# Moving the loads of the weights and the condition behind the first two chunks of x

## The chip, the cores and the metric

The kernel runs on one core of one Trainium2 chip. The metric is the time of one execution on the device in microseconds (us), the median of several runs; lower is better. The engines that matter here are TensorE (PE, with its weight loads as PEld), VectorE (DVE), ScalarE (ACT), SyncE (SP), and the 16 DMA engines of the core.

## The reference

The input x has 128 samples of 128 steps of 512 float32 numbers. A condition (128 x 512) goes through two dense layers and gives one gate of 512 numbers for each sample.

```python
h = silu(cond @ W1.T + b1)                 # 128 x 512
gate = sigmoid(h @ W2.T + b2)[:, None, :]  # one value per sample and feature
# a Haar transform of x over the 128 steps (log2(128) levels), its details and its
# average times gate, then the inverse transform
y = x + (x + inverse_haar(gate * haar(x))) # the gate is the same for all steps
```

The gate doesn't depend on the step, so the transform and its inverse cancel, and the result is `x * (2 + gate)`. That is what the kernel computes: one factor for each sample and feature, and one multiply over 33.6 MB of x that are read and written once.

## The kernel before

**The stream.** x is cut into 2 groups (g) of 64 samples. In each group the 128 partitions are 64 samples times 2 halves of the steps, and 8 chunks (s) of 8 steps each go over them. A chunk is 128 x 4096 float32, 2.1 MB. The tile `ring` has 8 slots, so the whole first group fits into it. SyncE (`block.sync`) issues the loads: first W1, the condition and W2 (L100 to L102), then the 8 chunks of group 0 (L104) without a wait, then the 8 chunks of group 1 (L109), each after the store of the chunk that held its slot (`chunk_stored`). All of these lie in one DMA queue, SP's, which the profile calls q1. VectorE multiplies chunk after chunk by `factor` in place (L218), each after its load (`chunk_loaded`). ScalarE issues the store of each chunk once it is scaled (L182), in its own DMA queue, q10. These stores hold 33.6 MB.

**The gate.** Before VectorE can scale the first chunk, `factor` has to be there. It comes from a chain over three engines. TensorE waits for the condition, turns it by 4 transposes (L126), then turns W1 by 16 (L132), and multiplies (`hidden_sum`, L140, 32 instructions). ScalarE takes the sigmoid (L171) while TensorE turns W2 (L149). VectorE copies turned tiles out of PSUM (L191, L194, L208) and forms `hidden` (L201). TensorE then forms `gate_sum` for group 0 and for group 1 (L157 for the bias, L160 for the product), ScalarE takes two sigmoids (L176), and VectorE adds 2 (L211, `factor`). VectorE and ScalarE run their instructions in the order written, so no chunk is scaled or stored ahead of this chain. The two biases are loaded in ScalarE's queue (L165, L166).

The parts that the change and the steps of the prediction touch:

Of the kernel before, what the change touches and what calls it, by code (L numbers as in the profile page):

```python
# [1 line left out]

# [8 lines left out]
CHUNK_STEPS = 8  # L31
GROUPS = 2
SLOTS = 8
DMA_DONE = 16


def gated_residual_program(nc, x, cond, w1, b1, w2, b2, out):
    B, N, D = x.shape
    BLOCKS = D // P
    SAMPLES = B // GROUPS  # L40
    assert B == P and D == BLOCKS * P and N == GROUPS * SLOTS * CHUNK_STEPS and GROUPS >= 2

    x_parts = x.rearrange("(g q) (h n) d -> g (q h) n d", g=GROUPS, h=GROUPS)
    out_parts = out.rearrange("(g q) (h n) d -> g (q h) n d", g=GROUPS, h=GROUPS)

    with ExitStack() as ctx:
        def sbuf(name, shape):
            return ctx.enter_context(nc.sbuf_tensor(name, shape, F32))
# [4 lines left out]
        def sem(name):  # L53
            return ctx.enter_context(nc.semaphore(name))


        ring = sbuf("ring", [P, SLOTS, CHUNK_STEPS, D])

# [27 lines left out]
        gate_summed, gate_set, factor_set = sem("gate_summed"), sem("gate_set"), sem("factor_set")  # L86
        chunk_loaded = [sem(f"chunk_loaded{s}") for s in range(SLOTS)]
        chunk_scaled = sem("chunk_scaled")
        chunk_stored = [sem(f"chunk_stored{s}") for s in range(SLOTS)]

        block = ctx.enter_context(nc.Block())

        def chunk(parts, g, s):

            return parts[bass.ds(g, 1), :, s * CHUNK_STEPS:(s + 1) * CHUNK_STEPS, :].rearrange("g p n d -> (g p) n d")

        @block.sync
        def _(sp):

            sp.dma_start(w1_rows[:, :, :], w1.rearrange("(p t) k -> p t k", t=BLOCKS)).then_inc(w1_loaded, DMA_DONE)  # L100
            sp.dma_start(cond_rows[:, :], cond).then_inc(cond_loaded, DMA_DONE)
            sp.dma_start(w2_rows[:, :, :], w2.rearrange("(t p) k -> p t k", p=P)).then_inc(w2_loaded, DMA_DONE)  # L102
            for s in range(SLOTS):
                sp.dma_start(ring[:, s, :, :], chunk(x_parts, 0, s)).then_inc(chunk_loaded[s], DMA_DONE)  # L104
            with sp.Fori(1, GROUPS) as g:
                for s in range(SLOTS):

                    sp.wait_ge(chunk_stored[s], g * DMA_DONE)
                    sp.dma_start(ring[:, s, :, :], chunk(x_parts, g, s)).then_inc(chunk_loaded[s], DMA_DONE)  # L109

# [130 lines left out]
```

## Time and profile before

| | before |
|---|---|
| median of 3 runs | 168.21 us (167.97 to 169.08) |
| span of the profiled execution | 166.7 us |
| time of the profiled execution beside its span | not recorded apart from the span |
| busy share of the span | DVE 47%, PE 14%, PEld 9%, ACT 2%, POOL 1% |
| DMA | 69.47 MB, mean 417 GB/s over the span |
| HBM read, written | 35.92 MB, 33.55 MB |

The span is the time from the first to the last instruction of the profiled execution. Against it stand the sums below; the median of the runs is 1.5 us above it. The page divides the span into 40 slices of 4.17 us; the digit in the DMA row is the mean busy share of the 16 DMA engines in tenths:

```profile
DVE  0160180019999999997809154280915428000000
DMA  5999999999999999999999999999999999999995
```

VectorE is busy without a break only from slice 9 on, and has gaps again in the second group. The DMA engines are at nine tenths or more in every slice but the first and the last.

### The profile page before, as it was taken

The numbers are of one execution on the slowest core, as the hardware profiler recorded it, in microseconds if no ns is written. First come the engines' busy times: TensorE is split into PE (matmuls) and PEld (weight loads), VectorE is DVE, ScalarE is ACT, GpSimd is POOL, SyncE is SP. The second block draws the span as 40 slices with busy tenths as digits, with TensorE's granted clock in tenths as the row PEclk, the third lists the DMA queues.
The fourth block names the chain that finished last, engine by engine and source line by source line (L and its number), as shares of the span: only waits on it lengthen the run. The fifth ranks groups of instructions, "written<-read, shape, count | busy, mean of one in ns | idle before, by whom it ended". The sixth has DMA issues, their size and how long they took to land.

```text
span 166.7 us, 361 instructions
## 1 busy us (share of the span) xinstructions
PE 23.7 (14%) x88; PEld 15.6 (9%) x88; DVE 78.3 (47%) x30; ACT 3.6 (2%) x7; POOL 0.8 (1%) x7
## 2 busy tenths in 40 slices
PE   0479619960000000000000000000000000000000
PEld 0479613320000000000000000000000000000000
DVE  0160180019999999997809154280915428000000
ACT  0000500110000000000000000000000000000000
POOL 2000000000000000000000000000000000000000
PEclk9999965997555555555555555555555555555555
DMA  5999999999999999999999999999999999999995
GB/s 167 313 457 440 421 421 429 433 437 433 413 437 429 429 437 440 425 425 429 437 429 437 433 425 433 429 433 433 437 433 425 433 429 429 437 433 433 429 429 236
DMA packets 5570, 69.47 MB, mean 417 GB/s; under 512 B 705, under 2 KB 705, under 8 KB 1346
## 3 DMA queue, kind: packets, MB, share of 16 engines
q1 hardware_dynamic: 3120, 35.91, 51.3%
q10 hardware_dynamic: 2450, 33.56, 47.1%
HBM read 35.92 MB, written 33.55 MB: 417 GB/s over the span
## 4 chain that ended last, share of the span: by engine, by line
DMA 41%; DVE 26%; PE 13%; ACT 2%; issue 2%; SPq 0%; DVEq 0%; ACTq 0%
DMA out<-ring 27%; DVE ring L218 22%; DMA ring<-in_x 11%; PE gate_sum L160 5%; PE hidden_sum L140 3%; DMA cond_rows<-in_cond 3%; PE turned L132 2%; PE gate_sum L157 2%; DVE w_t L208 1%; DVE hidden L201 1%; ACT L171 1%; ACT hidden_sigmoid L171 1%; PE turned_cond L126 1%; DVE factor L211 0%; DVE w_t L194 0%
## 5 line engine op out<-in xcount | busy, mean ns | idle before, releaser
L218 DVE TENSOR_TENSOR ring<-ring,factor 128x4096 f32<-128x4096 f32 x16 | 70.1, 4421 | 33.3 <-DMA ring<-in_x 33.0
L160 PE MATMUL gate_sum<-w_t,hidden 128*128 128x512 f32 x16 | 8.8, 702 | 0.0
L211 DVE TENSOR_SCALAR factor<-gate 128x1024 f32<-128x1024 f32 x1 | 0.7, 694 | 12.6 <-ACT gate L176 12.6
L140 PE MATMUL hidden_sum<-cond_t,w_t 128*128 128x128 f32 x32 | 5.5, 351 | 0.9 <-DVE w_t L194 0.9
L201 DVE SCALAR_TENSOR_TENSOR hidden<-hidden_sum,b_cols,hidden_sigmoid 128x256 f32<-128x256 f32 x4 | 1.7, 478 | 8.3 <-ACT hidden_sigmoid L171 8.3
L140 PEld LDWEIGHTS hidden_sum<-cond_t,w_t 128*128 128x128 f32 x32 | 5.3, 264 | 1.2 <-issue 1.2
L191 DVE COPY cond_t<-turned_cond 128x512 f32<-128x512 f32 x1 | 0.7, 692 | 7.8 <-PE turned_cond L126 7.8
L160 PEld LDWEIGHTS gate_sum<-w_t,hidden 128*128 128x128 f32 x16 | 3.5, 229 | 6.0 <-issue 6.0
L157 PE MATMUL gate_sum<-b_row,ones_row 1*128 1x512 f32 x4 | 3.2, 881 | 4.9 <-DVE w_t L208 4.9
L132 PE MATMUL turned<-identity,w_rows 128*128 128x128 f32 x16 | 3.6, 421 | 0.0
L132 PEld LDWEIGHTS turned<-identity,w_rows 128*128 128x128 f32 x16 | 3.4, 230 | 0.0
L194 DVE COPY w_t<-turned 128x512 f32<-128x512 f32 x4 | 2.8, 692 | 0.6 <-PE turned L132 0.6
L208 DVE COPY w_t<-turned 128x512 f32<-128x512 f32 x4 | 2.5, 681 | 0.0
L149 PE MATMUL turned<-identity,w_rows 128*128 128x128 f32 x16 | 2.1, 283 | 0.0
L126 PE MATMUL turned_cond<-identity,cond_rows 128*128 128x128 f32 x4 | 1.1, 428 | 6.6 <-DMA cond_rows<-in_cond 6.6
L149 PEld LDWEIGHTS turned<-identity,w_rows 128*128 128x128 f32 x16 | 2.0, 208 | 0.0
L171 ACT ACT_TABLE_LOAD x1 | 1.3, 1283 | 17.6 <-PE hidden_sum L140 17.6
L176 ACT ACTIVATE gate<-gate_sum 128x512 f32<-128x512 f32 x2 | 1.2, 597 | 15.5 <-PE gate_sum L160 15.5
L157 PEld LDWEIGHTS gate_sum<-b_row,ones_row 1*128 1x128 f32 x4 | 0.8, 244 | 5.8 <-issue 5.8
L126 PEld LDWEIGHTS turned_cond<-identity,cond_rows 128*128 128x128 f32 x4 | 0.7, 216 | 6.6 <-issue 6.6
L171 ACT ACTIVATE hidden_sigmoid<-hidden_sum,b_cols 128x128 f32<-128x128 f32 x4 | 1.1, 368 | 0.0
L117 POOL TENSOR_SCALAR_AFFINE_SELECT identity<-identity 128x128 f32<-128x128 f32 x1 | 0.3, 294 | 0.1
(6 smaller groups left out, 0.8 us busy)
## 6 DMA issues: line engine op xcount, KB each, us to landing
ring<-in_x SPq DMA_DIRECT2D x16, 2048.0 KB, 18.2
out<-ring ACTq DMA_DIRECT2D x16, 2048.0 KB, 34.8
w_rows<-in_L_cond_W SPq DMA_DIRECT2D x2, 1024.0 KB, 6.8
cond_rows<-in_cond SPq DMA_DIRECT2D x1, 256.0 KB, 5.3
b_cols<-in_L_cond_b ACTq DMA_DIRECT2D x1, 2.0 KB, 5.2
b_row<-in_L_cond_b ACTq DMA_DIRECT2D x1, 2.0 KB
```

The lines of the kernel that those rows point to most:

```text
L126: last = pe.transpose(turned_cond[:, c * B:(c + 1) * B], cond_rows[:, c * P:(c + 1) * P], identity[:, :])
L132: last = pe.transpose(turned[c][:, t * P:(t + 1) * P], w1_rows[:, t, c * P:(c + 1) * P], identity[:, :])
L140: last = pe.matmul(hidden_sum[:, t, :], w1_t[:, c, t, :], cond_t[:, c, :], start=(c == 0), stop=(c == BLOCKS - 1))
L149: last = pe.transpose(turned[t][:, m * P:(m + 1) * P], w2_strided[:, m, t, :], identity[:, :])
L157: pe.matmul(gate_sum[g][:, :], ones_row[:, :], b2_row[:, :], start=True, stop=False)
L160: last = pe.matmul(gate_sum[g][:, :], samples, w2_t[:, t, :], start=False, stop=(t == BLOCKS - 1))
L171: act.activation(hidden_sigmoid[:, t, :], hidden_sum[:, t, :], ACT.Sigmoid, bias=b1_cols[:, t:t + 1]).then_inc(sigmoid_set, 1)
L176: act.activation(gate[:, g, :], gate_sum[g][:, :], ACT.Sigmoid).then_inc(gate_set, 1)
L194: dve.tensor_copy(w1_t[:, c, :, :].rearrange("k t p -> k (t p)"), turned[c][:, :]).then_inc(w1_t_set, 1)
L201: dve.scalar_tensor_tensor(out=hidden[:, t, :, :], in0=hidden_sum[:, t, :].unsqueeze(2).to_broadcast([P, B, GROUPS]), scalar=b1_cols[:, t: ...
L208: dve.tensor_copy(w2_t[:, t, :], turned[t][:, :]).then_inc(w2_t_set, 1)
L218: dve.tensor_tensor(ring[:, s, :, :], ring[:, s, :, :], factor_steps, ALU.mult).then_inc(chunk_scaled, 1)
```

## The change

SyncE now issues the loads of chunks 0 and 1 of group 0 first, then W1, the condition and W2, and then chunks 2 to 7. The instructions are the same, with the same sizes, semaphores and queue; only their order on SyncE differs. Nothing changes on the other engines.

```diff
@@ -31,6 +11,7 @@
 CHUNK_STEPS = 8
 GROUPS = 2
 SLOTS = 8
+AHEAD = 2
 DMA_DONE = 16
@@ -97,10 +78,12 @@
         @block.sync
         def _(sp):
 
+            for s in range(AHEAD):
+                sp.dma_start(ring[:, s, :, :], chunk(x_parts, 0, s)).then_inc(chunk_loaded[s], DMA_DONE)
             sp.dma_start(w1_rows[:, :, :], w1.rearrange("(p t) k -> p t k", t=BLOCKS)).then_inc(w1_loaded, DMA_DONE)
             sp.dma_start(cond_rows[:, :], cond).then_inc(cond_loaded, DMA_DONE)
             sp.dma_start(w2_rows[:, :, :], w2.rearrange("(t p) k -> p t k", p=P)).then_inc(w2_loaded, DMA_DONE)
-            for s in range(SLOTS):
+            for s in range(AHEAD, SLOTS):
                 sp.dma_start(ring[:, s, :, :], chunk(x_parts, 0, s)).then_inc(chunk_loaded[s], DMA_DONE)
             with sp.Fori(1, GROUPS) as g:
                 for s in range(SLOTS):
```

## Rows read from the trace of the kernel before

**Rows 1.** The page's DMA queues: packets, MB, share of the 16 engines' span.

```profile
q1 hardware_dynamic: 3120, 35.91, 51.3%
q10 hardware_dynamic: 2450, 33.56, 47.1%
```

**Rows 2.** Windows: stretch, its length, busy us of PE, PEld, DVE, ACT, POOL, PEclk, DMA share, GB/s.

```profile
0.00:42.40 42.40, 23.68 (x88) 15.62 (x88) 12.81 (x16) 3.62 (x7) 0.84 (x7) 0.88 0.96 395
42.40:48.00 5.60, 0.00 (x0) 0.00 (x0) 5.60 (x2) 0.00 (x0) 0.00 (x0) 0.50 0.99 424
48.00:164.80 116.80, 0.00 (x0) 0.00 (x0) 59.88 (x14) 0.00 (x0) 0.00 (x0) 0.50 1.01 431
```

**Rows 3.** Chain of waits from the condition to `gate_sum`: start, length in us, what.

```profile
1.17 5.32 DMA cond_rows<-in_cond
6.63 1.09 PE turned_cond L126 x4
7.72 3.43 PE turned L132 x16
12.01 5.50 PE hidden_sum L140 x32
24.33 2.04 PE gate_sum L157 x2
31.41 1.05 PE gate_sum L157 x2
32.47 3.65 PE gate_sum L160 x8
```

**Rows 4.** Timeline, the scaling and storing: start, length, engine, line, operation, count.

```profile
37.79 26.10 DVE L218 TENSOR_TENSOR ring<-ring,factor 128x4096 f32<-128x4096 f32 x6 [0.33 <-DVE factor L211]
...
42.38 0.39 ACTq L182 DMA_DIRECT2D out<-ring  x1
```

**Rows 5.** Timeline, SyncE's issues of the first loads.

```profile
0.74 0.38 SPq L100 DMA_DIRECT2D w_rows<-in_L_cond_W  x1
...
1.65 0.43 SPq L102 DMA_DIRECT2D w_rows<-in_L_cond_W  x1
2.12 4.71 SPq L104 DMA_DIRECT2D ring<-in_x  x8
```

**Rows 6.** DMA issues near 0.74, 1.17 and 1.65 us: KB, us to landing.

```profile
w_rows<-in_L_cond_W SPq DMA_DIRECT2D x1, 1024.0 KB, 5.0
cond_rows<-in_cond SPq DMA_DIRECT2D x1, 256.0 KB, 5.3
w_rows<-in_L_cond_W SPq DMA_DIRECT2D x1, 1024.0 KB, 8.6
```

**Rows 7.** Line L104, issues 0 and 1: durations ns, starts, times to landing.

```profile
L104 SPq DMA_DIRECT2D ring<-in_x x2: 441/659/877, 2.1 to 3.0; - x2
...
DMA to landing us min/median/max: 13.1/15.1/17.1
```

**Rows 8.** Windows, the first 5 us and the last bytes.

```profile
0.00:5.00 5.00, 0.00 (x0) 0.00 (x0) 0.00 (x0) 0.00 (x0) 0.84 (x7) 1.00 0.62 208
164.00:165.00 1.00, 0.00 (x0) 0.00 (x0) 0.00 (x0) 0.00 (x0) 0.00 (x0) 0.50 0.69 295
```

**Rows 9.** DMA queues, window 45 to 46: the first packets of stores in q10.

```profile
q10 hardware_dynamic: 5, 0.08, 19.2%
```

**Rows 10.** TensorE's pace in the gate's chain (timeline, windows) and a VectorE copy.

```profile
8.61 0.69 DVE L194 COPY w_t<-turned 128x512 f32<-128x512 f32 x1 [0.16 <-PE turned L132]
17.33 2.08 PE L149 MATMUL turned<-identity,w_rows 128*128 128x128 f32 x16
26.00:28.00 2.00, 2.00 (x3) 0.84 (x3) 0.00 (x0) 0.00 (x0) 0.00 (x0) 0.50 1.02 434
27.31 0.34 PEld L160 LDWEIGHTS gate_sum<-w_t,hidden 128*128 128x128 f32 x1 [0.52 <-issue]
28.17 0.34 PEld L160 LDWEIGHTS gate_sum<-w_t,hidden 128*128 128x128 f32 x1 [0.52 <-issue]
```

## The prediction

> **What bounds the kernel now.** I read the page's slices first: every slice but the first and the last has the DMA engines at nine tenths or more, while VectorE is at 47%. So the time is bytes over a rate, and the question is whether the change opens a hole in that stream. The queue rows give the bytes: 35.91 MB in q1 and 33.56 MB in q10, 69.47 MB in all [rows 1]. The windows give the rate: 395 GB/s up to 42.4 us, 424 behind it, and 431 from 48.0 to 164.8 [rows 2]. Check: 42.4 x 0.395 = 16.75 MB are moved when the first store is issued; the other 52.72 MB at 0.431 MB/us take 122.3 us and end at 164.7, where the rate falls [rows 8]; the span ends 2.0 us later, at 166.7. The account closes. The chain of waits ends on VectorE and the stores, but behind 42 us it only retells that full DMA stream.
>
> The rows then show why there is no hole now. The first group's loads hold 35.91 - 8 x 2.097 = 19.13 MB (2.097 MB is a chunk). Up to 42.4 us 16.75 MB are done, so alone they would last 2.38 / 0.431 = 5.5 us more, to 47.9. Nothing else can be loaded then, since a slot comes free only by a store. The first store is issued at 42.38 [rows 4], and its first packets run in the window 45 to 46 [rows 9]. Stores thus come to the engines before the loads run out. The gate's chain is hidden, but with only a few us to spare.
>
> **The change, step by step.**
>
> 1. *The order.* SyncE's queue works in order: from issue plus time to landing, W1 lands at 0.74 + 5.0 = 5.7, the condition at 1.17 + 5.3 = 6.5, W2 at 1.65 + 8.6 = 10.3, chunk 0 at 2.12 + 13.1 = 15.2 and chunk 1 at 3.0 + 17.1 = 20.1 us [rows 5 to 7]. After the change two chunks stand ahead of the condition: 4.19 MB at 0.431 are 9.7 us; the two landings 4.9 us apart give 9.8. I take 9.7: the condition lands near 16.2, W1 before it. W2 lands some 3.8 us later, as now, about 20; it is wanted only behind `hidden_sum`, which would end near 27, so it costs nothing. W1's issue moves behind two issues of 0.44 and 0.88 us [rows 7], to about 2.1 us, long before its turn: nothing. Chunks 0 and 1 land near 8 and 13 instead of 15 and 20: worth nothing, since VectorE starts them only at 37.79, behind `factor` [rows 3, 4].
>
> 2. *The chain.* From the landing of the condition at 6.5 to the first scaling at 37.79 it takes 31.3 us, and no instruction of it changes. The first store's issue moves from 42.38 to 52.1.
>
> 3. *The start of the stores.* Now they start behind a full load queue, which hides their delay. After the change they meet idle engines. The delay from issue to an even flow isn't shown for that case in the middle of the kernel. The nearest row is the kernel's own start: 208 GB/s over 5 us are 1.04 MB, which at 0.431 would take 2.4 us, so the flow starts as if at 2.6, 1.8 us after the first issue at 0.74 [rows 5, 8]. The bounds are nothing, and the 3.3 us from 42.38 to late in the window 45 to 46 [rows 4, 9], where the engines still had q1's packets. I take 1.8 (engines idle, as they will be): flow of stores from 53.9. The Trainium skill ("DMA: Bandwidth & Descriptors", Specifications) gives a first-byte latency of about 0.6 us for this kind of queue; both rows here are longer, and by its figure the result would be 1.2 us lower.
>
> 4. *The hole.* The loads are done at 47.9 whatever their order, and the stores flow from 53.9: the engines idle for 6.0 us. As a sum over the whole: 9.7 (delay) - 3.7 (what the chain has to spare, 47.9 - 42.4 - 1.8) = 6.0.
>
> 5. *Can it be won back?* All bytes left at 53.9 are 33.56 + 16.78 = 50.34 MB; at 0.431 that is 116.8 us, end at 170.7, and with the 2.0 us of the tail 172.7, against 166.7. VectorE delivers a chunk in 26.10 / 6 = 4.35 us [rows 4], and a store takes 4.87, so the store queue doesn't run dry, and behind it the rate is at its ceiling as before. Only the second store, issued 4.35 us behind the first, is near the edge: if it took 3.3 us to its first byte while the first took 1.8, it would be 1.0 us late. Bounds: 0 to 1.0, I take 0. W2's slow landing (3.8 us for 1.05 MB) may be better or worse beside chunks; it would only move the end of the loads, and so the hole, not the end.
>
> 6. *TensorE's clock.* The chain isn't hidden any more, so its pace now counts. The granted clock reads 1.00 while TensorE idles at the start [rows 8], but the first transposes take 3.43 / 16 = 214 ns each, and those of W2 2.08 / 16 = 130 ns [rows 3, 10]. So it starts at the lower pace, whatever the record says, and a longer idle start should cost nothing: I take 0. The Trainium skill ("TensorE: Matmul & The Clock Gate", the two states) has an idle engine at 1.2 GHz by default; by that rule the start costs nothing either, whereas the recorded 1.00, taken at its word, would let the longer idle start end in a slower chain (rival B). In the gate's stage the granted clock is 0.50 (1.2 GHz) at 26 to 28 us, with weight loads 0.86 us apart [rows 10].
>
> Against the span the sum is +6.0 us. No time of the profiled execution is given beside its span; the runs' median is 1.5 us above it, and I keep that: 168.2 + 6.0 = **174.2 us**, with a step 3 between 172.4 and 175.7.
>
> **Rivals.**
>
> *A, not slower: TensorE catches up.* If its clock rose early and stayed up, all of the chain would run at the higher pace. The transposes of the condition and W1 would be 20 x 0.13 = 2.6 instead of 4.5, but four copies of 0.69 bound W1's part [rows 10]: -1.2. `hidden_sum` would take 32 x 0.13 = 4.2 instead of 5.5: -1.3. Group 0's part of `gate_sum` would take as long as group 1's, from 31.41 to 32.47 + 3.65 = 36.12, 4.7 us [rows 3], instead of 31.4 - 24.3 = 7.1: -2.4. Together -4.9, which leaves 1.1 us of the hole, and with a start of stores in 0.7 us none: 168.2 to 169.3. It decides when the chain gets 4.3 us or more shorter. Against it: TensorE idles about 5 us ahead of L157 in any case, and was slow after that here.
>
> *B, slower still: the clock stays down longer.* `hidden_sum` all at 214 ns is +1.4; group 0's 10 instructions of `gate_sum` at 0.86 are 8.6, +1.5; group 1's too, 8.6 against 4.7, +3.9. One stage late gives +2.9, all of them +6.8: 177.1 to 181.0. For it: nothing now hides a late rise. Against it: the clock had risen in both stages of this trace.
>
> *C, the order isn't what counts: the weights' packets pass the chunks*, since 16 engines work on the queue. Then the condition lands near 6.5 still, nothing moves, and 168.2 stays, or a little less by a better packed start (at most 1.8 us, if it cost nothing). Against it stand the five landings in issue order.
>
> *D, the change gains nothing and costs nothing because the ring still has loads to do.* It would need the loads to last to 53.9; they would need 2.6 MB more than they have. I give this no chance of its own.
>
> **How the numbers follow.** Forecast 0.80, A 0.07, B 0.09, C 0.04. About 1% (1.7 us) is what runs of this kernel can tell from no change. Slower by over 1% holds the forecast, B and 0.01 of A: 0.90; within 1%: the rest of A and half of C, 0.08; faster: the other half of C, 0.02. The forecast's own case runs from 172.4 (no delay of the stores) to 176.6 (3.3 us and a late second store), and some 1 us each way for where the clock rises. Leaving out A and C below and the longer part of B above, the range is 171.6 to 177.2.
>
> **What would show it.** The page's DMA row gets a hole near 48 to 54 us, in slices 11 and 12, and only there; windows over it show almost no GB/s. The condition lands at 16.2 (step 1), the first scaling starts at 47.5 (step 2), the first store is issued at 52.1 and flows 1.8 us later (step 3), and from there to the last byte it is 117 us (step 5). The first transposes stay at 214 ns (step 6). I am wrong if the first scaling moves by much less than 9.7 us, or if the DMA row has no hole, or if the rate behind it is above 431 GB/s.

## The result and the profile after

The changed kernel is slower: 173.8 us median (172.74 to 174.52, 4 runs) against 168.65 (167.97 to 169.85, 4 runs) for the kernel before; the ratio is 1.029, with a 95% interval of 1.025 to 1.034. That is 4.3 to 5.7 us. The profiled execution took 174.52 us with a span of 172.5, so 2.0 us lie around the span; it is the slowest of its four, whose spans go from 170.7 to 172.5.

The page's DMA rows, in slices of 4.31 us:

```profile
DMA  5999999999907999999999999999999999999997
GB/s 190 419 429 356 434 444 433 429 429 429 425 19 330 422 323 384 425 425 425 425 425 429 433 441 456 429 425 425 425 425 425 429 429 433 460 437 425 425 425 304
```

Slice 11 (47.4 to 51.7 us) is empty: that is the hole. Two more slices, 14 and 15, are full in the DMA row and yet move only 323 and 384 GB/s; in the page of the kernel before, no slice between the third and the last moves less than 413. Windows over that part (the columns are those of rows 2):

```profile
48.00:52.00 4.00, 0.00 (x0) 0.00 (x0) 4.00 (x2) 0.00 (x0) 0.00 (x0) 0.64 0.00 0
52.00:53.00 1.00, 0.00 (x0) 0.00 (x0) 1.00 (x1) 0.00 (x0) 0.00 (x0) 0.50 0.27 115
53.00:61.00 8.00, 0.00 (x0) 0.00 (x0) 8.00 (x3) 0.00 (x0) 0.00 (x0) 0.50 1.00 424
61.00:66.50 5.50, 0.00 (x0) 0.00 (x0) 5.50 (x2) 0.00 (x0) 0.00 (x0) 0.50 1.05 316
66.50:170.00 103.50, 0.00 (x0) 0.00 (x0) 50.96 (x12) 0.00 (x0) 0.00 (x0) 0.50 1.01 431
```

The loads end at 48.0, and 115 GB/s in the window 52 to 53 mean a flow at the full rate from about 52.7. The engines idle for 4.7 us. From 61.0 to 66.5 they are busy at 316 GB/s, which loses (431 - 316) x 5.5 / 431 = 1.5 us; behind that the rate is that of [rows 2].

How the loads land now, by issue (KB, us to landing; issued at 0.74, 1.64, 2.11 and 2.77 us):

```profile
ring<-in_x SPq DMA_DIRECT2D x1, 2048.0 KB, 7.4
...
w_rows<-in_L_cond_W SPq DMA_DIRECT2D x1, 1024.0 KB, 14.0
cond_rows<-in_cond SPq DMA_DIRECT2D x1, 256.0 KB, 14.1
w_rows<-in_L_cond_W SPq DMA_DIRECT2D x1, 1024.0 KB, 16.6
```

Chunk 0 is there at 8.1 us, W1 at 15.6, the condition at 16.2 and W2 at 19.4, in the order of issue as in [rows 5 to 7]. The chain of waits behind the condition, piece by piece, for [rows 3]:

```profile
2.11 14.12 DMA cond_rows<-in_cond
...
16.37 1.08 PE turned_cond L109 x4
17.45 3.43 PE turned L115 x16
...
21.74 5.47 PE hidden_sum L123 x32
...
34.02 2.04 PE gate_sum L140 x2
36.06 5.04 PE gate_sum L143 x8
41.10 1.05 PE gate_sum L140 x2
42.15 3.65 PE gate_sum L143 x8
```

Every piece has the length of before, and all start 9.7 us later. The timeline of what follows, for [rows 4]:

```profile
47.47 17.43 DVE L201 TENSOR_TENSOR ring<-ring,factor 128x4096 f32<-128x4096 f32 x4 [0.33 <-DVE factor L194]
52.06 9.01 ACTq L165 DMA_DIRECT2D out<-ring  x3
58.45 0.33 SPq L92 DMA_DIRECT2D ring<-in_x  x1
```

The first store is issued at 52.06 and flows at 52.7, 0.6 to 0.7 us later; the first load of group 1 is issued at 58.45.

### The profile page after: what moved, and what is told of

The parts are those of the page before. It is cut to its first block, busy times and chain, and to the rows that moved or that the text cites. A ratio compares the mean times of both kernels' runs of the same rounds, so it can differ in the third digit from the quotient of the medians.

```text
span 172.5 us, 361 instructions
## 1 busy us (share of the span) xinstructions
PE 23.6 (14%) x88; PEld 15.6 (9%) x88; DVE 78.2 (45%) x30; ACT 3.6 (2%) x7; POOL 0.8 (0%) x7
## 4 chain that ended last, share of the span: by engine, by line
DMA 42%; DVE 24%; PE 13%; issue 3%; ACT 2%; SPq 1%; DVEq 0%; ACTq 0%
DMA out<-ring 25%; DVE ring L201 21%; DMA ring<-in_x 9%; DMA cond_rows<-in_cond 8%; PE gate_sum L143 5%; PE hidden_sum L123 3%; PE turned L115 2%; PE gate_sum L140 2%; DVE w_t L191 1%; DVE hidden L184 1%; ACT L154 1%; ACT hidden_sigmoid L154 1%; PE turned_cond L109 1%; SPq L82 0%; DVE factor L194 0%
```

## The experiments

The theory: the delay of the first store beyond what the chain has to spare (4.9 us, from 42.38 + 0.7 to 48.0) is idle time of the DMA engines and comes back whole. The rivals: the order of the loads costs something by itself; the stream's disturbance behind the hole is the cost; each chunk ahead costs a fixed share.

### The delay without the order: late_factor

```diff
 # the order of loads of the kernel before; DELAY = 13
+for k in range(DELAY):
+    dve.tensor_scalar_add(factor[:, :, :], gate[:, :, :], 2.0).then_inc(factor_set, 1)
+    dve.wait_ge(factor_set, k + 1)
 dve.tensor_scalar_add(factor[:, :, :], gate[:, :, :], 2.0).then_inc(factor_set, 1)
-dve.wait_ge(factor_set, 1)
+dve.wait_ge(factor_set, DELAY + 1)
```

> The kernel before with its order of loads, but VectorE forms the factor 14 times in a row instead of once: 13 more instructions of 0.69 us and their waits, some 9.5 to 10 us. Theory (only the late factor costs): the first store is issued near 52, the loads end at 48, and the time is that of the changed kernel, ratio 1.025 to 1.033. Rival (the order of the loads costs by itself): ratio 1.000 to 1.01.

Measured: 173.68 us, ratio 1.029 (1.026 to 1.033), span 172.3. The timeline and the windows:

```profile
51.79 26.34 ACTq L183 DMA_DIRECT2D out<-ring  x7
```

```profile
48.00:52.00 4.00, 0.00 (x0) 0.00 (x0) 4.00 (x2) 0.00 (x0) 0.00 (x0) 0.50 0.03 12
52.00:61.00 9.00, 0.00 (x0) 0.00 (x0) 9.00 (x3) 0.00 (x0) 0.00 (x0) 0.50 0.96 408
61.00:66.00 5.00, 0.00 (x0) 0.00 (x0) 5.00 (x2) 0.00 (x0) 0.00 (x0) 0.50 1.05 305
66.00:170.00 104.00, 0.00 (x0) 0.00 (x0) 51.20 (x12) 0.00 (x0) 0.00 (x0) 0.50 1.00 429
```

With the loads in the old order, and only the factor 9.4 us late, the hole, the slow patch and the whole loss are those of the changed kernel. The new order isn't needed for any of it.

### The order without the delay: split_after

VectorE forms the factor of each group just ahead of that group's scaling, so that group 0 doesn't wait for group 1's gate; the order of loads is that of the changed kernel.

```diff
-dve.wait_ge(gate_set, GROUPS)
-dve.tensor_scalar_add(factor[:, :, :], gate[:, :, :], 2.0).then_inc(factor_set, 1)
-dve.wait_ge(factor_set, 1)
-with dve.Fori(0, GROUPS) as g:
+for g in range(GROUPS):
+    dve.wait_ge(gate_set, g + 1)
+    dve.tensor_scalar_add(factor[:, g, :], gate[:, g, :], 2.0).then_inc(factor_set, 1)
+    dve.wait_ge(factor_set, g + 1)
     ... # the scaling of the 8 chunks, as before
```

> The changed kernel, but the factor of group 0 is formed as soon as its own gate is there, and scaling starts with it, not behind group 1's gate: 4.7 us for group 1's products and 0.35 us of the addition leave the path, so the first scaling starts near 42.4 and the first store is issued near 47. Theory (hole = 48.0 less the first store's issue and 0.7): no hole, ratio against the kernel before 1.000 to 1.003. Rival (the order of the loads costs by itself, or something behind the hole): 1.02 to 1.03.

Measured: 168.28 us, ratio 0.999 (0.996 to 1.002). The timeline has the first store at 46.45. Windows over the end of the loads and behind it, and two pieces of the chain of waits:

```profile
47.00:48.00 1.00, 0.00 (x0) 0.00 (x0) 1.00 (x1) 0.00 (x0) 0.00 (x0) 1.00 1.12 475
48.00:49.00 1.00, 0.00 (x0) 0.00 (x0) 1.00 (x1) 0.00 (x0) 0.00 (x0) 1.00 0.92 393
56.00:60.00 4.00, 0.00 (x0) 0.00 (x0) 4.00 (x2) 0.00 (x0) 0.00 (x0) 0.50 1.02 328
```

```profile
21.37 3.82 PE hidden_sum L123 x32
34.05 6.70 PE gate_sum L143 x8
```

No hole, and no loss: the order by itself costs nothing that the runs show. The chain is 5.6 us shorter than in the changed kernel, 5.0 of it by the edit and most of the rest because `hidden_sum` starts 0.4 us earlier. `hidden_sum` itself ran 3.82 us instead of 5.47, but that was lost again: group 0's product took 6.70 us instead of 5.04.

A slow patch is there at 56 to 60 (328 GB/s, 1.0 us lost). The ratio shows nothing of it. But the ten times stand in two clumps, four of them, with the profiled 169.14, at 169.0 to 169.6 us and six at 167.6 to 168.6. The distance is about that of the patch; whether the four are those that have it isn't shown, since only one execution has a profile.

### How much the chain has to spare: ahead1, ahead4

```diff
-AHEAD = 2
+AHEAD = 1   # ahead4: 4
```

> One chunk ahead instead of two: the first store is issued 4.9 us later than before, near 47.3. Theory (the time is the hole in the DMA stream: delay less what the chain has to spare): with a start delay of the stores of 0.7 us, as the changed kernel showed at 52.06 to 52.7, the chain has 4.9 us to spare, the hole is 0, and the time is that of before, ratio 1.000 within 0.003. With the 1.8 us of the prediction it would be 1.2 us slower (1.007). Rival (every chunk put ahead costs its share, 2.9 us by the changed kernel's span): ratio 1.017.

Measured: 169.42 us, ratio 1.0035 (1.0001 to 1.0068), span 166.6. It is less of a test than meant, since the chain was shorter here too. Its chain of waits and its timeline:

```profile
16.73 3.82 PE hidden_sum L123 x32
```

```profile
41.26 4.42 DVE L201 TENSOR_TENSOR ring<-ring,factor 128x4096 f32<-128x4096 f32 x1 [0.33 <-DVE factor L194]
```

The first scaling moved by 3.5 us, not 4.9. That is within what the chain has to spare by either start delay, 0.7 or 1.8 us, and the stream has no hole, so the run doesn't decide between the two delays. The rival by shares (1.017) is out. The interval lies just above 1.000, though, and where that third of a per cent comes from isn't shown.

> Four chunks ahead: delay 19.5 us, less 4.9 to spare: a hole of 14.6 us from 48.0, ratio 1.087, and 1.094 if the extra loss of 1.0 us behind the hole in the changed kernel's profile comes with every hole. The rival by shares (2.9 us a chunk) gives +11.6 us, 1.069.

Measured: 184.17 us, ratio 1.095 (1.089 to 1.102), span 181.1. Windows:

```profile
48.00:60.60 12.60, 6.33 (x14) 2.11 (x12) 5.27 (x3) 1.19 (x2) 0.00 (x0) 0.90 0.00 0
60.60:70.00 9.40, 0.00 (x0) 0.00 (x0) 9.40 (x3) 0.00 (x0) 0.00 (x0) 0.50 0.92 390
70.00:75.00 5.00, 0.00 (x0) 0.00 (x0) 5.00 (x2) 0.00 (x0) 0.00 (x0) 0.50 1.08 315
```

The first store is issued at 60.61, so the hole is 60.61 + 0.7 - 48.0 = 13.3 us, and the span grew by 14.4. In the changed kernel it is 4.7 and 5.8. The rival by shares (1.069) is out here too. In both pairs of profiles 1.1 us come on top of the hole, but that isn't a fixed cost: the profiled execution of ahead4 was the shortest of its four, that of the changed kernel the longest, and by the medians it is about 0.5 us in the changed kernel and 2 in ahead4. Both times the slow patch begins some 9 us behind the first store's issue.

### Which weight matters: w2_behind, own_queue

```diff
 # w2_behind: W1 and cond, then the two chunks, then W2, chunks 2 to 7
+sp.dma_start(w1_rows, ...)
+sp.dma_start(cond_rows, ...)
 for s in range(AHEAD):
     sp.dma_start(ring[:, s, :, :], ...)
-sp.dma_start(w1_rows, ...)
-sp.dma_start(cond_rows, ...)
 sp.dma_start(w2_rows, ...)
```

> Only W2's load stands behind the two chunks, W1 and the condition ahead of them as in the kernel before. Theory (only the condition and W1 open the gate's chain): W2 lands near 20 us instead of 10.3, its transposes end near 22.2 instead of 19.4, and VectorE copies it from 21.8 as before, each copy behind its transposes: the first scaling moves by at most 1 us, ratio 1.000. Rival (chunks of x in front of any weight disturb the stream): up to 1.029.

Measured: 167.91 us, ratio 0.9955 (0.9925 to 0.9985). Timeline:

```profile
19.39 2.19 PE L132 MATMUL turned<-identity,w_rows 128*128 128x128 f32 x16 [1.74 <-DMA w_rows<-in_L_cond_W]
21.86 2.48 DVE L191 COPY w_t<-turned 128x512 f32<-128x512 f32 x4
```

TensorE waits 1.74 us for W2, and it costs nothing, since VectorE is busy with `hidden` until 21.9 anyhow. Two chunks of x ahead of W2 alone are free; what costs is that they are ahead of W1 and the condition.

```diff
 # own_queue: the two chunks first on SyncE; the weights go to ScalarE's queue
 act.dma_start(b2_row, ...)
+act.dma_start(w1_rows, ...)
+act.dma_start(cond_rows, ...)
+act.dma_start(w2_rows, ...)
```

> The two chunks are first in SyncE's queue, but W1, the condition and W2 go into ScalarE's queue, behind the biases. If the queue's order is what delays them, they now share the engines with the chunks: W1 and the condition land near 8 to 14 us instead of 15.6 and 16.2, and the first scaling starts earlier than in the changed kernel unless W2, in packets of 2 KB against 16 KB of the chunks, comes late (it holds the chain if it lands behind 26). Either way the first scaling and the time follow hole = first store's issue + 0.7 - 48.0; ratio 1.000 if W2 lands by 22, up to 1.05 if it lands near 36.

Measured: 187.74 us, ratio 1.11 (1.107 to 1.116). Its profile is of the longest of its four executions (span 188.3 us, the others 184.5 to 185.9). DMA issues near 2.1 and 3.0 us, the timeline, and the window behind the end of the loads:

```profile
cond_rows<-in_cond ACTq DMA_DIRECT2D x1, 256.0 KB, 20.0
...
w_rows<-in_L_cond_W ACTq DMA_DIRECT2D x1, 1024.0 KB, 40.5
```

```profile
43.59 3.69 PE L129 MATMUL turned<-identity,w_rows 128*128 128x128 f32 x16 [12.53 <-DMA w_rows<-in_L_cond_W]
```

```profile
48.00:68.40 20.40, 13.37 (x20) 4.74 (x20) 5.88 (x4) 1.20 (x2) 0.00 (x0) 0.75 0.00 0
```

The condition lands at 22.1, later than behind the two chunks in their own queue (16.2), and W2 at 43.5, later than even the poor end of the expectation (36). The first store is issued at 67.81, so the formula gives a hole of 67.81 + 0.7 - 48.0 = 20.5 us, and the window has 20.4 us without a byte. The median lies 19.2 us above the kernel before. The theory thus holds for a third size of hole, to about 1 us.

Beside a stream of 16 KB rows, the queue with rows of 2 KB gets far less than half of the bytes. The DMA queues in the window 16.5 to 22.1, in which the condition flows:

```profile
q1 hardware_dynamic: 145, 2.11, 89.4%
q10 hardware_dynamic: 144, 0.26, 12.4%
```

The two queues move equally many packets, and these are about a row long (14.6 and 1.8 KB on average), so the bytes go as the lengths of the rows: 2.11 MB against 0.26. The Trainium skill ("DMA: Bandwidth & Descriptors", Queues, rings and completion order) says that an engine takes turns between its queues packet by packet, and the trace agrees.

### The slow patch: again, hold_reload

The changed kernel once more, with its own profile:

> The changed kernel as it is, a second profile. The hole near 48 to 52.7 us must be there again (4.7 us). If the slow patch at 61 to 66.5 us (315 GB/s, 1.5 us lost) belongs to the change, it is there again too, and the span stays near 172.5; if it was chance, the span is near 171.2. Ratio 1.029.

Measured: 173.89 us, ratio 1.029 (1.023 to 1.034), span 172.8. Windows:

```profile
48.00:53.00 5.00, 0.00 (x0) 0.00 (x0) 5.00 (x2) 0.00 (x0) 0.00 (x0) 0.63 0.00 0
61.00:67.00 6.00, 0.00 (x0) 0.00 (x0) 6.00 (x2) 0.00 (x0) 0.00 (x0) 0.50 1.00 306
```

Hole and patch are both there again; the patch is no chance.

```diff
 # the changed kernel, ahead of the loads of group 1
+sp.wait_ge(chunk_stored[2], DMA_DONE)
 with sp.Fori(1, GROUPS) as g:
```

> The changed kernel, but SyncE waits for the third store before it issues the first load of group 1 (at about 67 instead of 58.4 us). VectorE needs that chunk at 82 us, so the wait costs nothing by itself. In every kernel with a hole, the profile shows a slow patch from 9 to 14 us behind the first store's issue (about 315 GB/s, some 1.1 to 1.5 us lost), where the third store and the first reload are issued 2.3 us apart. Theory: the patch comes from the reload's start beside a short store queue; without the reload it is gone, the span is near 171.2, ratio 1.022. Rival: it belongs to the stores alone (the third store starts late), the patch stays at 61 to 66 us, ratio 1.029.

Measured: 174.4 us, ratio 1.033 (1.029 to 1.038), span 172.0. The first reload is issued at 67.67 instead of 58.45. Windows:

```profile
53.00:61.00 8.00, 0.00 (x0) 0.00 (x0) 8.00 (x3) 0.00 (x0) 0.00 (x0) 0.50 1.01 426
61.00:66.00 5.00, 0.00 (x0) 0.00 (x0) 5.00 (x2) 0.00 (x0) 0.00 (x0) 0.50 1.01 429
66.00:78.00 12.00, 0.00 (x0) 0.00 (x0) 12.00 (x4) 0.00 (x0) 0.00 (x0) 0.50 0.99 373
```

Stores alone run at 429 GB/s through 61 to 66 us, so they aren't slow by themselves; the loss has moved behind the reload's issue, (431 - 373) x 12 / 431 = 1.6 us. The patch belongs to the start of the reload. But it wasn't taken away, so my expectation of 1.022 was wrong.

The queues tell more of what happens in it. The changed kernel in the window 63 to 66.5, then the kernel before in 57.5 to 61, where its own first reload starts to flow:

```profile
q1 hardware_dynamic: 64, 1.05, 96.6%
q10 hardware_dynamic: 16, 0.00, 0.3%
```

```profile
q1 hardware_dynamic: 50, 0.82, 54.8%
q10 hardware_dynamic: 55, 0.64, 42.8%
```

In the changed kernel the first half chunk of the reload flows alone: the store queue moves nothing to speak of for 3.5 us. Up to then it has moved some 4.2 MB, two whole stores, so it is the third store that starts late, 5.8 us after its issue at 60.73. The packets also take longer, 96.6% of 16 engines over 3.5 us for 64 packets, which is 0.85 us each against 0.61 in the kernel before, so the engines show as busy at a low rate. In the kernel before both queues flow side by side. The traces of again, late_factor, ahead4 and split_after show the same silence of the stores, and hold_reload shows it at 72 to 74. Why the stores stop is open: the kernel before issues its first reload at 54.3 us with no such patch, and ahead1 at 53.6 has none either, while split_after at 53.7 has one.

### A version that is faster: w2_long, best, best_a

```diff
 # w2_long: the kernel before, with
-w2.rearrange("(t p) k -> p t k", p=P)
+w2.rearrange("(p t) k -> p t k", t=BLOCKS)
-dve.tensor_copy(w2_t[:, t, :], turned[t][:, :])
+dve.tensor_copy(w2_t[:, t, :].rearrange("k (p m) -> k m p", m=BLOCKS),
+                turned[t][:, :].rearrange("k (m p) -> k m p", m=BLOCKS))
 # best_a: w2_long and the split factor; best: that, and W2 behind the two chunks
```

> The kernel before, but W2 is loaded with 8 KB in a row for each partition as W1 is, instead of four rows of 2 KB; the copy out of PSUM puts the columns back in order. In the trace of before W2 took 3.8 us for 1.05 MB against 2.4 at the stream's rate. If that is the price of the short packets, the stream gets 1.4 us shorter and the ratio is 0.992; if the slow landing was only the start of the stream, it is 1.000. The chain has enough to spare for either (the strided copies may cost some tenths of a us).

Measured: 168.02 us, ratio 0.996 (0.994 to 0.998). W2's issue and landing, and the window 5 to 10 us of w2_long:

```profile
w_rows<-in_L_cond_W SPq DMA_DIRECT2D x1, 1024.0 KB, 7.3
```

```profile
5.00:10.00 5.00, 3.42 (x16) 3.45 (x17) 1.97 (x3) 0.00 (x0) 0.00 (x0) 1.00 1.04 433
```

W2 lands at 9.0 instead of 10.3 us. The window has 433 GB/s; the kernel before has this there:

```profile
5.00:10.00 5.00, 3.37 (x16) 3.40 (x17) 1.92 (x3) 0.00 (x0) 0.00 (x0) 1.00 1.04 363
```

That is 0.35 MB, 0.8 us at the stream's rate, and 0.5 us by the medians, 0.7 by the ratio (0.4%), reach the time. So in these two traces the rows of 2 KB cost about 0.8 us, not 1.4. The rate falls in the same way where W2 passes later: at 15 to 20 us it is 374 GB/s in w2_behind, with rows of 2 KB, and 426 in best, with rows of 8 KB.

> Together: W1 and the condition first, then the two chunks, then W2 in rows of 8 KB, and the factor of group 0 on its own. The hole stays away by some 8 us to spare. The gain of the long rows (0.996) and of W2 behind the chunks (0.9955) come from the same place if both are the start of the stream: then 0.995; if they add up, 0.992.

Measured: 167.91 us, ratio 0.9955 (0.993 to 0.998).

> The kernel before with W2 in rows of 8 KB and the factor of group 0 on its own. Scaling starts 5 us earlier, which the full DMA stream should hide: ratio 0.996, as with the long rows alone. Rival (the earlier stores help the stream): 0.992.

Measured: 168.09 us, ratio 0.996 (0.994 to 0.999). All three stand together near 0.996: the gains don't add up, and scaling earlier is worth nothing once the DMA stream is full. They beat both kernels, by 0.4% and by over 3%. The 0.4% isn't all the rows' doing: w2_behind gains as much and keeps the rows of 2 KB. And part of it is that the longest executions are missing: of the 69 executions of the kernel before that were timed beside all these runs, 16 took 169.2 us or more, while of the 36 of w2_long, best and best_a none took more than 168.51. Why is open.

## Why the prediction was right

The time predicted was 174.2 us; it is 173.8, inside the range, and in the order of cases the forecast's. By its steps:

1. *The order: right.* The condition lands at 16.2 us as predicted, and chunks 0 and 1 at 8.1 and 13.1. Rival C is out.
2. *The chain: right.* First scaling at 47.47 (predicted 47.5), first store at 52.06 (52.1). late_factor and split_after show from both sides that the loss comes with this delay and not with the order.
3. *The start of the stores: mis-sized.* I took 1.8 us from the kernel's start, and it was 0.7; in late_factor and ahead4 it was 0.6 and 0.8, read in the same way from 262 GB/s in the windows 52 to 53 and 61 to 62. The ramp of the kernel's first microseconds was the wrong row for a queue in the middle of a run. The Trainium skill ("DMA: Bandwidth & Descriptors", Specifications) has a figure of about 0.6 us, which I set aside; the traces agree with it for idle engines.
4. *The hole: 1.3 us too long*, nearly all for that reason, 6.0 us predicted and 4.7 measured. The chain has 4.9 us to spare, not 3.7.
5. *Nothing is won back: right; nothing more is lost: wrong.* The ceiling of 431 GB/s holds behind 66.5 us, but the slow patch loses 1.5 us that no row of before showed. I had looked for trouble at the second store, at 0 to 1.0 us. It isn't late, the window 53 to 61 has 424 GB/s; it is the third that doesn't flow while the reload starts.
6. *TensorE's clock: right in the changed kernel*, whose pieces all have the length of before. The first transposes take 214 ns each behind 16 us of idling as behind 6.6. But the pace of the chain isn't fixed. In ahead1, ahead4, split_after, w2_long, best_a, own_queue and hold_reload `hidden_sum` took 3.82 us instead of 5.5, and hold_reload runs the changed kernel's instructions up to there, so it differs from one execution to the next. That is rival A's faster `hidden_sum`. But group 0's product then took 5.5 to 6.7 us instead of 5.0, which is rival B's slower stage: split_after has 2.04 + 6.70 = 8.7 us for its 10 instructions, where B had 8.6. The two together are 1.2 us shorter at most (ahead1 and ahead4) and equal in split_after. So A and B each came true in part, and nearly cancelled.

In sum, the spans of the two profiled executions differ by 5.8 us, where 6.0 were predicted: 1.3 too much in steps 3 and 4, 1.5 too little in step 5. That leaves 0.4, and it lies at the end: I kept the tail of 2.0 us behind the stream, and in the changed kernel's trace the last bytes move just before 171.25, 1.25 us ahead of the span's end. So the mechanism was right, but that the total fits better than its terms is luck.

There is more of it in the time. I added 6.0 us to 168.2, the median of three executions; a fourth has moved that median to 168.65. By the medians the change costs 173.8 - 168.65 = 5.15 us, 0.85 less than I forecast, while the times 174.2 and 173.8 are only 0.4 apart.

## What to carry to other kernels

Where a stream of loads fills all buffers and a side chain must end before the first buffer is given back, compare two times: the end of those loads, and the end of the chain plus the start of the first store. As long as the second is the earlier one, the order in the queue is nearly free (0.35% in ahead1, nothing in split_after); beyond it, each microsecond of the chain's delay costs about a microsecond of the kernel, in holes of 4.7, 13.3 and 20.5 us. So what opens such a chain goes first in the queue, and what it needs only later (W2 here) can go behind bulk data; moving small loads to another queue didn't let them pass here, since their rows were short.

## What was not expected of the hardware

- Both DMA directions run at 424 to 431 GB/s alone and mixed, but a reload that started while stores ran cost 1.0 to 1.7 us in six traces (after, again, late_factor, split_after, ahead4, hold_reload). In the changed kernel the stores stood still for 3.5 us meanwhile, with the engines shown as busy.
- A store's start delay is 0.6 to 0.8 us on idle engines (three traces) and 3.3 us in the kernel before, where the other queue is full.
- 1.05 MB in rows of 2 KB landed 40.5 us after their issue when their queue shared the engines with rows of 16 KB, and 8.6 us after it in one queue. From 16.5 to 22.1 us each queue moved as many packets as the other, 145 and 144, whatever the rows' lengths.
- The granted clock reads 1.00 (2.4 GHz) over idling and first transposes alike, while those run at 214 ns each and later ones at 130: at the start of these traces, the pace tells more than the record.
